# The second mixture's products move to GpSimd, two attention tiles at a time, and a repeated listing of the woven stages

## Chip, core and metric

One Trainium2 chip, one of its cores. The metric is the device time of one execution in microseconds (us); lower is better. The engines are TensorE (PE), VectorE (DVE), ScalarE (ACT), GpSimd (POOL) and SyncE (SP), which issues the DMAs here.

## The reference, cut to what matters

Four sequences (b = 0 to 3) of 1024 tokens of 128 numbers, in float32. Two layers:

```
xn = layernorm(x)
x  = x + attention0(xn) + mixture0(xn)            # 1 causal head; 16 experts of 64 + 1 shared, top 2
xn = layernorm(x)
x  = x + attention1(xn) + block1(xn)              # attention1: 16 heads of 8, not causal
# block1: res = xn + small causal attention (16 heads of 4) @ w_up
#         result = res + mixture1(rmsnorm(res))   # 8 experts of 256, top 2
mixture(t) = sum over experts of  route[t, e] * ((silu(t @ wg[e]) * (t @ wu[e])) @ wd[e])
attention0(t): softmax(t @ R @ t.T, causal) @ t
```

## The kernel before, in words

The tokens of a sequence are 8 tiles of 128 (T = 8) or two halves of 512 (HALF). For each sequence the program has two kinds of stages.

*The windows* (`Plan.windows`): eight groups of four heads, scores and exponentials and values. They are not touched by the change.

*The woven stages* (`Weave`, between two windows): here run together the tiles of the first attention and the first mixture of sequence b (`tiles`, `mixture` with which = 0), the closing of sequence b-1 (`closing`: output projections, residual, routing of the second mixture), the second mixture of sequence b-1 (`mixture` with which = 1), and the opening of the second layer of sequence b (`opening`: sums, norm, q, k, v, their bfloat16 parts written to DRAM, stacks read back, then the 32 "pieces" of the first head group with a row maximum each, the maxima split on GpSimd and placed by DMA, and then the first unit of the window). Stage 0 has no closing and no second mixture; the last stage has only a closing and a second mixture.

The program of each engine is written out at build time. `Weave` holds operations with an engine, an assumed duration and what they follow; `run` lists them: of those that can start within 0.1 us of the earliest, it takes the one with the longest tail of work behind it, and appends it to its engine's queue. A queue runs in that order; only semaphore waits hold an instruction.

*A step of a mixture* (18 for the first, 32 for the second): `gate` (PE, L1515; bank 0 or 3 in turn), its Tanh or Silu (ACT, L1284 or L1286) into `sg`, `up` (PE, L1525; one bank, U_BANK), the gated value `gu` (DVE, L1018 and L1024, or L1029 for the second mixture), the product `hid = gu * spread_w` with the route weights of one expert spread over the partitions (DVE, L1041), and `down` (PE, L1490), which adds into Y_BANK. `sg`, `gu` and `hid` have two buffers each; `spread_w` has four, filled by SP's DMAs (L777 for the second mixture) from `scratch_r`, where the routes were stored (L767). After each half `mixed` adds Y_BANK to x or writes `res` (L1054, L1056). The PE's `gate` of step 0 or 1 of a mixture waits in the kernel before for the gated value of the step in front of it:

```
                elif n >= 2:
                    pe.wait_ge(s["sg_ready"], k - 1)
                elif k:
                    pe.wait_ge(s["gu_ready"], k)
```

*A tile of the first attention* is a chain: scores (PE, L1435 and a mask, L1436), row maximum (DVE, L974), Exp with its sum (ACT, L1266), transposes (PE, L1441), their copy (ACT, L1272), values (PE, L1447), scaled add into x (DVE, L984). All of it passes through one PSUM tensor, FRONT_PS = ps[3], so the scores of tile t wait for L984 of tile t-1. The closing uses the PSUM tensor XA = ps[2], from its first transposes (L1648) over L1654, L1663, L1474, L1675 to the projection (L1680), which DVE adds to x (L1211), then the bias (L1214). The opening's split of q and k is L1070 (DVE) and L1293 (ACT).

## Time and profile before

| | us |
|---|---|
| runs | 2183.12, 2181.83, 2180.65 (median 2181.83) |
| the profiled execution | 2177.56, with a span of 2175.7 |
| PE busy | 2039.7 (94%) |
| DVE busy | 1549.5 (71%) |
| ACT busy | 1214.4 (56%) |
| GpSimd busy | 131.7 (6%) |
| stage 0 (span 0 to the first unit of a window) | 0 to 181.2 |
| woven stages 1, 2, 3 | 494.5 to 700.6, 1017.6 to 1223.4, 1540.5 to 1746.2 |
| last stage | 2058 to 2175.7 |

How to read it: busy time is the union of an engine's instructions; the span is from the first to the last instruction. An engine at 94% is near its end, but the share is a mean over stages, so each stage has to be looked at by itself.

### The profile page before, as it was taken

How to read it: one execution, taken by the hardware profiler on the slowest of the kernel's cores; microseconds unless marked ns; L12 is line 12 of the kernel's file. 1: busy time of each engine (PE TensorE's matmuls, PEld its weight loads, DVE VectorE, ACT ScalarE, POOL GpSimd, SP SyncE). 2: the span in 40 equal slices, each digit the busy share in tenths (PEclk: the TensorE clock that was granted, in tenths of full speed). 3: DMA queues.
4: the chain of work that ended last, by engine and by line, in shares of the span. 5: the costliest groups of instructions: out<-in, count | busy, mean ns of one | idle time of the engine just before them, and what ended most of it. 6: DMA issues, size and time to landing. Idle time of an engine off the chain costs nothing. (4 is left out here: it accounts for less than half of the span.)

```text
span 2175.7 us, 33722 instructions
## 1 busy us (share of the span) xinstructions
PE 2039.7 (94%) x11936; PEld 945.4 (43%) x11936; DVE 1549.5 (71%) x2807; ACT 1214.4 (56%) x2325; POOL 131.7 (6%) x251
## 2 busy tenths in 40 slices
PE   6869999989999999998989999999999999999889
PEld 4622333436665233344655423343565632334355
DVE  5678887746788887663779888774577988777155
ACT  2224777773532677776351467777444166777621
POOL 2000011100000000110000000110000000111000
PEclk9957999999999999999999999999999999999989
DMA  5160101002171100001145010010106301000011
GB/s 191 35 174 1 30 16 38 20 2 69 45 193 35 30 16 25 17 17 31 49 123 130 11 30 16 26 31 2 60 20 184 74 17 20 22 25 17 2 47 41
DMA packets 66632, 105.17 MB, mean 48 GB/s; under 512 B 11137, under 2 KB 20289, under 8 KB 66081
## 3 DMA queue, kind: packets, MB, share of 16 engines
q1 hardware_dynamic: 66464, 103.03, 17.6%
q8 instruction: 94, 1.54, 0.3%
q14 instruction: 74, 0.60, 0.1%
HBM read 79.26 MB, written 22.94 MB: 47 GB/s over the span
## 5 line engine op out<-in xcount | busy, mean ns | idle before, releaser
L1339 ACT ACTIVATE prob<-ps 128x512 f32<-128x512 f32 (+3 forms) x1792 | 867.4, 555 | 354.6 <-PE ps L1605 265.0
L1145 DVE TENSOR_REDUCE row_max<-ps 128x1 f32<-128x1024 f32 x512 | 606.6, 1219 | 106.3 <-PE ps L1574 105.6
L1605 PE MATMUL ps<-q_stack,k_stack 96*128 96x512 bf16 (+4 forms) x1792 | 553.0, 363 | 24.9 <-ACT prob L1339 17.0
L1574 PE MATMUL ps<-k_stack,q_stack 96*128 96x512 bf16 (+4 forms) x1792 | 534.9, 372 | 28.0 <-DMA q_stack<-scratch_q 15.6
L1142 DVE CUSTOM_DVE_ANT_0 tmp<-ps,const_b 128x128 f32<-128x128 f32 (+7 forms) x512 | 371.4, 756 | 131.3 <-PE ps L1574 118.1
L1630 PE MATMUL ps<-prob,v_ones 128*32 128x512 f32 (+3 forms) x3584 | 436.9, 559 | 2.5 <-ACT prob L1339 2.5
L1605 PEld LDWEIGHTS ps<-q_stack,k_stack 96*128 96x128 bf16 (+1 forms) x1792 | 172.5, 98 | 360.8 <-ACT prob L1339 231.8
L1574 PEld LDWEIGHTS ps<-k_stack,q_stack 96*128 96x128 bf16 (+1 forms) x1792 | 152.8, 99 | 376.3 <-DVE row_max L1142 94.9
L1490 PEld LDWEIGHTS ps<-wd,prob 128*128 128x128 f32 (+1 forms) x1600 | 207.1, 193 | 78.0 <-issue 66.3
L1286 ACT ACTIVATE prob<-ps 128x512 f32<-128x512 f32 x128 | 76.4, 597 | 288.5 <-PE ps L1515 287.9
L1490 PE MATMUL ps<-wd,prob 128*128 128x128 f32 (+1 forms) x1600 | 213.2, 278 | 3.3 <-DVE prob L1041 3.3
L1041 DVE TENSOR_TENSOR prob<-prob,spread_w 128x512 f32<-128x512 f32 x192 | 131.9, 688 | 52.2 <-PE ps L1490 50.5
L1515 PE MATMUL ps<-tT,wg 128*128 128x512 f32 x256 | 136.8, 617 | 14.1 <-DVE prob L1029 14.1
L1525 PE MATMUL ps<-tT,wu 128*128 128x512 f32 x256 | 134.6, 608 | 0.0
L1630 PEld LDWEIGHTS ps<-prob,v_ones 128*32 128x32 f32 x3584 | 70.6, 108 | 136.3 <-ACT prob L1339 75.9
L1029 DVE TENSOR_TENSOR prob<-prob,ps 128x512 f32<-128x512 f32 x128 | 87.4, 683 | 31.5 <-issue 12.6
L1607 PE MATMUL ps<-const_b 128*128 128x128 bf16 x512 | 103.5, 219 | 0.0
L1160 DVE RECIPROCAL rsum_g<-ps 128x16 f32<-128x16 f32 x64 | 16.5, 258 | 120.1 <-PE ps L1640 115.6
L1284 ACT ACTIVATE prob<-ps 128x512 f32<-128x512 f32 (+1 forms) x72 | 42.9, 596 | 82.5 <-PE ps L1515 81.7
L1515 PE MATMUL ps<-xT,wg 128*128 128x512 f32 x144 | 74.3, 598 | 0.3 <-DVE prob L1024 0.3
L1515 PEld LDWEIGHTS ps<-tT,wg 128*128 128x128 f32 x256 | 47.8, 194 | 56.9 <-issue 49.9
L853 POOL TENSOR_SCALAR m_rest<-row_max 128x32 f32<-128x32 f32 x32 | 9.3, 292 | 1041.9 <-DVE row_max L1145 849.8
(169 smaller groups left out, 1510.3 us busy)
## 6 DMA issues: line engine op xcount, KB each, us to landing
spread_w<-scratch_r SPq DMA_DIRECT2D x128, 128.0 KB, 2.9
spread_w<-scratch_r SPq DMA_DIRECT2D x64, 256.0 KB, 3.5
k_stack<-scratch_k SPq DMA_DIRECT2D x48, 256.0 KB, 6.8
q_stack<-scratch_q SPq DMA_DIRECT2D x48, 256.0 KB, 7.7
scratch_k<-tmp SPq DMA_DIRECT2D x36, 256.0 KB, 2.8
k_stack<-scratch_k SPq DMA_DIRECT2D x96, 64.0 KB, 2.2
q_stack<-scratch_q SPq DMA_DIRECT2D x96, 64.0 KB, 2.3
scratch_k<-tmp SPq DMA_DIRECT2D x36, 128.0 KB, 2.8
```

The lines of the kernel that those rows point to most:

```text
L1029: dve.tensor_tensor(gu[k % 2][0:m, :], sg[k % 2][0:m, :], bank(U_BANK)[0:m, :], ALU.mult).then_inc(s["gu_ready"], 1)
L1041: dve.tensor_tensor(hid[k % 2][:], gu[k % 2][:], spread_w[load % SPREADS][:], ALU.mult).then_inc(s["hid_ready"], 1)
L1142: dve.tensor_tensor_reduce(masked[r % 2][:, 0:keys], ring_pair(r)[:, 0:keys], mask_wide[:, S - keys:], 1.0, -3e38, ALU.add, ALU.max, nm[G ...
L1145: dve.tensor_reduce(nm[G % 2][:, t, j:j + 1], ring_pair(r)[:], AX_X, ALU.max).then_inc(s["ring_used"], 1)
L1339: act.activation(p_slot(v, j)[:, lo - at:hi - at], bank(UNIT_BANKS[u % 3])[:, 0:hi - lo], ACT.Exp, scale=SCALES[kind_of(G)]).then_inc(s["p ...
L1490: ins = pe.matmul(bank(Y_BANK)[:, t * D:(t + 1) * D], hid[k % 2][0:m, t * P:(t + 1) * P], wd[0:m, c * D:(c + 1) * D], start=(c, t) == (0, ...
L1515: pe.matmul(bank(G_BANKS[n % 2])[0:m, :], wg[:, c * P:c * P + m], xT[:, tok], start=True, stop=True).then_inc(s["gate_psum"], 1)
L1525: pe.matmul(bank(U_BANK)[0:m, :], wu[:, c * P:c * P + m], xT[:, tok], start=True, stop=True).then_inc(s["up_psum"], 1)
L1574: ins = pe.matmul(ring_pair(r)[:, lo:hi], queries(G, j)[:, t * P:(t + 1) * P], keys(G, j)[:, lo:hi], start=True, stop=True)
L1605: ins = pe.matmul(dst[:, 0:hi - lo], keys(G, j)[:, kc * P:(kc + 1) * P], queries(G, j)[:, lo:hi], start=True, stop=True)
L1607: ins = pe.matmul(dst[:, 0:P], mask_q, ident_b, start=False, stop=True, skip_group_check=True)
L1630: ins = pe.matmul(bank(V_BANK)[CW * j:CW * (j + 1), lo - at:hi - at], v_st[G % 2][:, kc, j, :], p_slot(v, j)[:, lo - at:hi - at], start=kc ...
```

## The change

1. The products of the second mixture (`spread` with which = 1) are issued by GpSimd, not by DVE. The first mixture's stay on DVE. They are in GpSimd's queue beside `maxima` and `stage_v`.
2. Tiles 0 to 3 of the first attention use the two halves of FRONT_PS in turn, tiles 4 and 6 all of FRONT_PS, tiles 5 and 7 all of XA. Tile t then waits for the tile that last had its space (`TILES_FREE`); tile 5 also for the closing of sequence b-1 to be done with XA (`po_used`, `rt_ready`). The transposed probabilities go back into the tile's own buffer `p0[t % 2]`.
3. `Weave.run` lists the operations up to 12 times, forwards and, from the ends so found, backwards, whose starts are the next turn's priorities; the best modelled end is kept. The plan is told of the engine and 1.1 us for the products, of shorter times for several PE operations, and of waits of the second mixture's first steps one by one (gate 0, gate 1, first product and first down each behind what they need of the first mixture, not all behind its last `mixed`).
4. In the program, `gate` of step 0 or 1 waits for the gated value of the step before the one in front of it, which frees its bank, its `sg` buffer being free then too.

The core of the diff (a few assumed times of `closing` and `opening`, and `heads`, are left out):

```diff
+    def listed(self, after, value):
+
+        waiting = [len(list_) for list_ in after]
+        follows = [[] for _ in self.ops]
+        for k, list_ in enumerate(after):
+            for d in list_:
+                follows[d].append(k)
+        at, free, out = [0.0] * len(self.ops), {}, []
+        can = [k for k, n in enumerate(waiting) if n == 0]
+        while can:
+            start = {k: max(at[k], free.get(self.ops[k][0], 0.0)) for k in can}
+            first = min(start.values())
+            k = max((k for k in can if start[k] <= first + 0.1), key=lambda k: (value[k], -k))
+            engine, _, took, _, lands = self.ops[k]
+            can.remove(k)
+            out.append((k, start[k]))
+            free[engine] = start[k] + took
+            for n in follows[k]:
+                at[n] = max(at[n], start[k] + took + max(lands, self.ops[n][4] if after is not self.after else 0.0) + (LAT if self.ops[n][0] != engine else 0.06))
+                waiting[n] -= 1
+                if not waiting[n]:
+                    can.append(n)
+        return out, max(start + self.ops[k][2] + self.ops[k][4] for k, start in out)
...
+    def run(self, plan, turns=12):
+
+
+        ops = self.ops
+        self.after = [sorted(set(op[3])) for op in ops]
+        follows = [[] for _ in ops]
+        for k, list_ in enumerate(self.after):
+            for d in list_:
+                follows[d].append(k)
+        value = [0.0] * len(ops)
         for k in reversed(range(len(ops))):
-            tail[k] += ops[k][2] + ops[k][4]
-            for d in ops[k][3]:
-                tail[d] = max(tail[d], tail[k] + LAT)
-        while len(self.end) < len(ops):
-            heads = [(max(at, self.free.get(ops[k][0], 0.0)), k) for at, k in self.heads()]
-            first = min(heads)[0]
-            _, k = max((tail[k], -k) for at, k in heads if at <= first + 0.1)
-            start = next(at for at, n in heads if n == -k)
-            self.free[ops[-k][0]] = self.place(plan, -k, start)
+            value[k] = ops[k][2] + ops[k][4] + max([LAT + value[n] for n in follows[k]], default=0.0)
+        best = None
+        for _ in range(turns):
+            out, end = self.listed(self.after, value)
+            if best is None or end < best[1]:
+                best = out, end
+            ends = [0.0] * len(ops)
+            for k, start in out:
+                ends[k] = start + ops[k][2] + ops[k][4]
+            back, _ = self.listed(follows, ends)
+            for k, start in back:
+                value[k] = start + ops[k][2]
+        for k, start in best[0]:
+            self.free[ops[k][0]] = self.place(plan, k, start)
...
+    def tiles(w, b, closed=None):
+
+        valued = []
         def do(engine, stage, took, *after):
             return w.op(engine, ("front", b, stage), took, *after)
-        used = do("ACT", "encode", 1.1, do("PE", "encode", 2.0))
-        out = []
+        coded = do("ACT", "encode", 1.1, do("PE", "encode", 1.73))
+        out, before = [], [None] * 7
         for t in range(T):
-            top = do("DVE", f"scores{t}", 0.15 + 0.13 * (t + 1), do("PE", f"scores{t}", 0.1 + 0.24 * (t + 1), used))
-            p = do("ACT", f"scores{t}", 0.45 + 0.115 * (t + 1), top)
-            turned = do("ACT", f"turn_p{t}", 0.18 + 0.115 * (t + 1), do("PE", f"turn_p{t}", 0.12 * (t + 1), p))
-            used = do("DVE", f"values{t}", 0.65, do("PE", f"values{t}", 0.25 * (t + 1), turned))
-            out.append(used)
+            freed = [out[t - 2]] if t >= 2 and t != 5 else []
+            if t == 4:
+                freed.append(out[3])
+            elif t == 5:
+                freed.append(closed)
+            at = [do("PE", f"scores{t}", 0.1 + 0.24 * (t + 1), coded, *freed, before[0])]
+            at.append(do("DVE", f"scores{t}", 0.15 + 0.13 * (t + 1), at[0], before[1]))
+            at.append(do("ACT", f"scores{t}", 0.45 + 0.115 * (t + 1), at[1], before[2], valued[t - 2] if t >= 2 else None))
+            at.append(do("PE", f"turn_p{t}", 0.12 * (t + 1), at[2], before[3]))
+            at.append(do("ACT", f"turn_p{t}", 0.18 + 0.115 * (t + 1), at[3], before[4]))
+            valued.append(do("PE", f"values{t}", 0.25 * (t + 1), at[4], before[5]))
+            out.append(do("DVE", f"values{t}", 0.65, valued[-1], before[6]))
+            before = at + [valued[-1], out[-1]]
         return out
...
-                at = do("PE", "gate", 0.88, last(taken, 2), last(taken) if n == 1 else None, last(scaled, 2), last(ups), xT if n == 0 else None, *(freed if n == 0 else ()))
+                at = do("PE", "gate", 0.865, last(taken, 2), last(scaled, 2), last(ups), xT if n == 0 else None, freed[n] if freed and n < 2 else None)
                 gates.append(do("ACT", "gate", 0.6, at, last(scaled, 2), last(gates)))
-                ups.append(do("PE", "up", 0.0 if which == 0 and n % C0 == C0 - 1 else 0.88, at, last(scaled), mixed if n == 0 else None))
+                ups.append(do("PE", "up", 0.0 if which == 0 and n % C0 == C0 - 1 else 0.865, at, last(scaled), freed[1] if freed and n == 0 else None))
...
-                hids.append(do("DVE", "spread", 0.7 if at else 0.05, scaled[-1], last(downs), last(hids), *at))
+                hids.append(do(("DVE", "POOL")[which], "spread", (0.7, 1.1)[which] if at else 0.05, scaled[-1], last(downs), last(hids), freed[2] if freed and n == 0 else None, *at))
...
-                downs.append(w.op("PE", ("down", b, which, n - 1), 1.05, hids[n - 1], last(out), last(downs)))
+                downs.append(w.op("PE", ("down", b, which, n - 1), 0.9, hids[n - 1], last(out), last(downs), freed[3] if freed and n == 1 else None))
...
-        return out, (taken[-1], scaled[-1], hids[-1], out[-1]), loads
+        return out, (scaled[-2], scaled[-1], downs[-1], out[-1]), loads
...
-        tiled = tiles(w, b)
+        tiled = tiles(w, b, project)
         mixed, freed, loads = mixture(w, b, 0, None, None if b else stored, (None, None), loads)
         if b:
-            mixture(w, b - 1, 1, xT, routed, (joined, joined), loads, freed, mixed[-1])
+            mixture(w, b - 1, 1, xT, routed, (joined, joined), loads, freed)
...
+        def tile_ps(t):
+
+            if t < T // 2:
+                return FRONT_PS[:, t % 2 * HALF:(t % 2 + 1) * HALF]
+            return (FRONT_PS, XA)[t % 2][:]
+
+        TILES_FREE = [0, 0, 1, 2, 4, 4, 5, 6]
...
+            def spread(b, which, n):
+                k, load = plan.step0[b, which] + n, plan.load_of(b, which, n)
+                if n == 0:
+                    pool.wait_ge(s["hid_ready"], k)
+                pool.wait_ge(s["gu_ready"], k + 1)
+                pool.wait_ge(spread_loaded[load % SPREADS], spread_count(load))
+                pool.wait_ge(s["down_done"], k - 1)
+                pool.tensor_tensor(hid[k % 2][:], gu[k % 2][:], spread_w[load % SPREADS][:], ALU.mult).then_inc(s["hid_ready"], 1)
+
             for what, *how in plan.of("POOL"):
-                if what == "maxima":
+                if what == "spread" and how[1] == 1:
+                    spread(*how)
...
-                    dve.tensor_reduce(nmax0[:, t:t + 1], FRONT_PS[:, 0:(t + 1) * P], AX_X, ALU.max, negate=True).then_inc(s["max0_ready"], 1)
+                    dve.tensor_reduce(nmax0[:, t:t + 1], tile_ps(t)[:, 0:(t + 1) * P], AX_X, ALU.max, negate=True).then_inc(s["max0_ready"], 1)
...
+                    if t >= 2:
+                        act.wait_ge(s["o0_psum"], b * T + t - 1)
+                    act.activation(p0[t % 2][:, 0:keys], tile_ps(t)[:, 0:keys], ACT.Exp, bias=nmax0[:, t:t + 1],
                                    accum_out=sum0[:, t:t + 1]).then_inc(s["p0_ready"], 1)
...
-                    act.activation(pT0[:, 0:keys], FRONT_PS[:, 0:keys], ACT.Copy).then_inc(s["pt_ready"], 1)
+                    act.activation(p0[t % 2][:, 0:keys], tile_ps(t)[:, 0:keys], ACT.Copy).then_inc(s["pt_ready"], 1)
...
-                    else:
-                        pe.wait_ge(s["o0_used"], b * T + t)
+                    if TILES_FREE[t]:
+                        pe.wait_ge(s["o0_used"], b * T + TILES_FREE[t])
+                    if b and t == T // 2 + 1:
+                        pe.wait_ge(s["po_used"], b)
+                        pe.wait_ge(s["rt_ready"], b)
...
-                elif k:
-                    pe.wait_ge(s["gu_ready"], k)
+                elif k >= 2:
+                    pe.wait_ge(s["gu_ready"], k - 1)
```

## Rows read from the trace of the kernel before

**Rows 1.** Windows by stage: length, engines busy (x instructions), granted clock, DMA share, GB/s.

```profile
0.00:181.20 181.20, 134.31 (x545) 70.21 (x546) 122.24 (x207) 42.67 (x65) 15.88 (x19) 0.80 0.41 120
494.50:700.60 206.10, 196.92 (x984) 127.48 (x983) 159.32 (x274) 70.38 (x107) 3.44 (x8) 0.98 0.33 89
1017.60:1223.40 205.80, 196.92 (x992) 127.41 (x991) 159.77 (x275) 70.38 (x107) 3.43 (x8) 0.98 0.34 89
...
2058.00:2175.70 117.70, 101.48 (x474) 66.28 (x472) 59.98 (x119) 27.85 (x43) 0.00 (x0) 0.92 0.15 41
```

**Rows 2.** Windows inside woven stage 1: tiles and first mixture, then opening, then pieces.

```profile
494.50:572.50 78.00, 76.69 (x424) 53.44 (x423) 55.15 (x122) 28.16 (x51) 0.00 (x0) 1.00 0.18 55
572.50:620.00 47.50, 39.93 (x185) 24.25 (x183) 33.95 (x68) 26.14 (x31) 1.33 (x1) 0.93 0.51 145
620.00:700.60 80.60, 80.29 (x377) 49.79 (x378) 70.23 (x85) 16.08 (x25) 2.11 (x7) 0.98 0.38 89
```

**Rows 3.** Waits of PE in woven stage 1: total us, times, longest.

```profile
PE ps L1515 <- DVE prob L1029: 4.4, 1, 4.4
PE ps L1574 <- DMA q_stack<-scratch_q: 3.0, 1, 3.0
PE ps L1424 <- DVE routeT L1007: 1.3, 1, 1.3
PE ps L1680 <- ACT tmp L1379: 0.3, 1, 0.3
```

**Rows 4.** Timeline of woven stage 1: start, length, engine, line, xcount, idle before.

```profile
539.80 1.56 PE L1435 MATMUL ps<-xT,tmp 128*128 128x512 f32 x4
...
573.62 2.05 PE L1680 MATMUL ps<-wo,tmp 128*128 128x128 f32 x16 [0.25 <-ACT tmp L1379]
...
575.51 1.02 PE L1525 MATMUL ps<-tT,wu 128*128 128x512 f32 x2
...
580.93 2.05 PE L1515 MATMUL ps<-tT,wg 128*128 128x512 f32 x2 [4.40 <-DVE prob L1029]
...
592.33 0.68 DVE L1041 TENSOR_TENSOR prob<-prob,spread_w 128x512 f32<-128x512 f32 x1
```

**Rows 5.** Windows behind PE's waits in stages 1 and 2 (columns as before).

```profile
580.93:587.42 6.49, 6.49 (x20) 3.39 (x21) 1.93 (x3) 3.22 (x5) 0.00 (x0) 0.54 0.04 5
1105.10:1111.50 6.40, 6.26 (x22) 3.17 (x23) 2.78 (x3) 4.08 (x6) 0.00 (x0) 0.73 0.04 5
...
620.10:624.00 3.90, 3.88 (x13) 2.45 (x14) 2.94 (x3) 0.60 (x1) 0.00 (x0) 0.62 1.05 196
```

**Rows 6.** Line of the row maxima in woven stage 1: durations in ns, first and last start.

```profile
L1145 DVE TENSOR_REDUCE row_max<-ps x33: 1212/1217/1225, 620.8 to 700.5; 128x1 f32<-128x1024 f32 x33
```

**Rows 7.** GpSimd's lines, ns minimum, median, maximum; one copy with DVE beside it.

```profile
L846 POOL COPY v_ones<-v_tok x16: 398/402/1330, 113.5 to 1852.2; 128x256 f32<-128x256 f32 x16
L857 POOL TENSOR_TENSOR m_rest<-m_rest,m_parts x32: 244/247/532, 174.0 to 2017.6; 128x32 f32<-128x32 f32 x32
...
595.76 2.55 DVE L1070 TENSOR_TENSOR tmp<-tmp 128x1024 f32<-128x1024 f32 x2
...
595.91 1.33 POOL L846 COPY v_ones<-v_tok 128x256 f32<-128x256 f32 x1 [145.42 <-DVE v_tok L1103]
```

**Rows 8.** Timeline of the last stage: closing, first product and down, one steady step.

```profile
2058.75 1.96 PE L1648 MATMUL ps<-const_f,v_tok 128*64 128x128 f32 x16 [0.61 <-DVE v_tok L1163]
...
2090.56 1.23 DVE L1214 TENSOR_TENSOR x<-x,bias_vo 128x1024 f32<-128x1024 f32 x1
...
2091.70 0.68 DVE L1041 TENSOR_TENSOR prob<-prob,spread_w 128x512 f32<-128x512 f32 x1
...
2092.53 2.05 PE L1490 MATMUL ps<-wd,prob 128*128 128x128 f32 x8 [3.33 <-DVE prob L1041]
...
2105.73 0.69 DVE L1041 TENSOR_TENSOR prob<-prob,spread_w 128x512 f32<-128x512 f32 x1 [1.11 <-PE ps L1490]
...
2109.76 1.05 PE L1490 MATMUL ps<-wd,prob 128*128 128x128 f32 x8
```

**Rows 9.** Window of the tiles and first mixture in stage 0 (same columns).

```profile
24.00:97.00 73.00, 69.25 (x360) 46.42 (x358) 48.30 (x93) 24.30 (x44) 0.34 (x1) 1.00 0.22 73
```

More of the change, by code:

```diff
@@ L297, in op @@
         return len(self.ops) - 1
-    def heads(self):
-        for k in [k for todo in self.todo.values() for k in todo]:
-            engine, item, took, after, lands = self.ops[k]
-            if all(d in self.end for d in after):
-                yield max([0.0] + [self.end[d] + self.ops[d][4] + (LAT if self.ops[d][0] != engine else 0.06) for d in after]), k
     def place(self, plan, k, at):
@@ L1226, in _ @@
                     up(*how)
-                elif what == "spread":
+                elif what == "spread" and how[1] == 0:
                     spread(*how)
```

29 lines of the change are left out of this document (13 added, 16 removed).

## Prediction

> **What bounds the kernel now.** I read the windows by stage first [rows 1], because the page's 94% for PE is a mean over stages. The change touches only the woven stages, stage 0 and the last stage. Woven stages 1 to 3 last about 206 us each, PE is busy in 196.9 us of that and its granted clock is 0.98; DVE is busy in 159.3 and ACT in 70.4. So PE sets the length of a woven stage, and what can be won is PE's idle time, 206.1 - 196.9 = 9.2 us a stage, and what its lower clock costs. Stage 0 has a lower mean clock and much more idle time, but most of that lies in its opening, a chain the change doesn't shorten.
>
> Inside stage 1 [rows 2] the first part, tiles and first mixture, keeps PE busy for 76.7 of 78.0 us at full clock. The last part, pieces and second mixture, keeps it busy for 80.3 of 80.6. All that is missing is in the middle: 39.9 of 47.5 us. PE's waits name it [rows 3]: 4.4 us in which a gate matmul (L1515) waits for the gated value L1029, and 3.0 us in which the first piece waits for its stack from DRAM; these two, with 1.3 and 0.3 and smaller ones, are the 9.2. Stages 2 and 3 show the same pattern. The timeline has the first place [rows 4]: the up matmul starts at 575.51 and lasts 1.02, then nothing until 580.93. The gate is step 1's and its wait (`gu_ready, k`) is for step 0's value, which DVE had behind the routing, the projection and the norm.
>
> A wait of PE costs more than itself. The gate that follows takes 2.05 us where the up before it took 1.02, and in the 6.49 us behind the wait the granted clock is 0.54 in stage 1, and 0.73 over 6.40 us in stage 2 [rows 5]: PE went from 2.4 to 1.2 GHz after it had idled and came back while it was kept busy. The loss is length times (1 - clock): 6.49 x 0.46 = 3.0 us and 6.40 x 0.27 = 1.7 us. Behind the wait for the stack it is 3.90 x 0.38 = 1.5 us.
>
> What is not the bound: the chain of the opening. The pieces start at 620.8 [rows 6]; 32 maxima of 1.217 us are 39 us, and some 10 us of splitting and placing follow, so the first unit could start near 670. It starts at 700.6, because PE does the second mixture in between. This chain has 30 us of room.
>
> **The change part by part.** *Products to GpSimd.* DVE loses 32 products of 0.69 us [rows 8], 22 us a stage. In the last part of the stage DVE is busy in 70.2 of 80.6 us, yet PE hardly waits there [rows 2], so this alone gives nothing there; in the middle part it takes a few products out of the queue in which L1029 stands. What one costs on GpSimd the trace doesn't show. From below: a copy of 256 columns takes 402 ns and a product of 32 columns 247 ns [rows 7], 0.69 ns a column, so 512 columns take 0.247 + 480 x 0.00069 = 0.58 us if a second input is free. From above: the copy's whole time, doubled for the columns and again for the second input, 1.61 us. I take 1.15, between the two. Is it hidden? In the steady step of the last stage a product starts at 2105.73, when the down two steps earlier has freed its buffer, and is used by the down at 2109.76 [rows 8]: ends of 2106.42 now and 2106.9 then are both early, with 2.9 us left; at 1.61 still 2.4. GpSimd needs 1.15 of each 2.61 us step. Behind the product in GpSimd's queue stand the six small instructions of `maxima`, for which the first unit waits; a product ahead of them costs at most 1.15 us once, in the chain with 30 us of room. SP's loads now wait for GpSimd's products instead of DVE's; four buffers and 2.61 us steps cover half a microsecond.
>
> The Trainium skill (GPSIMD Engine Reference, Elementwise — side-by-side cycle accounting) gives GpSimd about 2.6 cycles an element for a product of two inputs and 4497 ns for 2048 columns; the estimate for 512 columns is 1.1 us, and the sum would be the same by it.
>
> *Contention.* The copy of 402 ns took 1330 beside two L1070, DVE instructions that read two SBUF tensors; these took 2.55 us together instead of 2 x 1.216 [rows 7]; it happened in 4 of the 16 copies, once a stage. So a GpSimd instruction waited 0.93 us and DVE 0.1 to 0.2 us. The second mixture's products will meet DVE's two-input instructions of the opening (six L1070, six for the rotation, bias and join: 14). None of them is on PE's path as long as PE has other work, and the opening's chain has 30 us of room: I take 0. Uncovered, 14 delays of at most one product are 14 x 1.15 = 16 us a stage. The row maxima and L1029 read PSUM, and no copy beside them was longer than 404 ns.
>
> *Gates as banks need.* The gate of step 1 (0.86 us of PE time, a third of the 2.61 us step) no longer waits for L1029; of the 4.4 us it can fill 0.9. The next thing that is late is up 1, which still needs it, so the rest has to come from the order. From below this part is worth 0.9 us a stage, from above the wait and its low clock, 7.4 in stage 1.
>
> *Tiles.* Two at a time they no longer wait for each other. In stages 1 to 3 PE has no idle time there [rows 2], so nothing is won directly. But XA must be free before tile 5. Before, tile 5's scores began at 539.80, and the projection, which ends the closing, only at 573.62 [rows 4]. The closing alone takes from 2058.75 to 2090.56 [rows 8], 31.8 us, so it can be done by 494.5 + 31.8 = 526.3 if it is let go first; the new plan must put it ahead of tile 5. Then the second mixture's routes, whose first product was at 592.33 [rows 4], are known some 20 to 30 us earlier, and DVE's routing work no longer stands in front of L1029. That is what takes the 4.4 us away, together with a listing that sees PE's load (the backward pass counts it, the tail of the old one doesn't). In stage 0 [rows 9] PE idles 3.75 us in this part; I take 1.5 of it, bounds 0 and 3.75.
>
> *The wait for the stack* (3.0 us and 1.5 of low clock) is a DMA chain that the plan assumes too short; the edit doesn't aim at it. PE stalls only because the piece stands too early in its queue. I take a third: bounds 0 and 4.5.
>
> *The last stage.* The first product stood behind the bias add on DVE: it started at 2091.70, and PE waited 3.33 us for it [rows 8]. On GpSimd it starts when the spread weights are there, near 2089.7, and ends near 2090.9, 1.5 us earlier than 2092.4. The last product is 0.5 us later, and the down, the add and the store follow it. Net -1.0; the other 31 steps are PE's 2.61 us each and don't change.
>
> **The sum.** Wait: 3 x 4.4 = 13.2. Low clock behind it: 3.0 + 1.7 + 1.7 (stage 3 like 2) = 6.4. Stack: 3 x 1.5 = 4.5. Stage 0: 1.5. Last stage: 1.0. Together 26.6 us. The profiled execution took 2177.56 around its span of 2175.7 and would take 2151.0; it lies 4.3 below the median of the runs shown, 2181.83, which becomes 2155.2.
>
> **The rivals.**
> *More than that:* the new listing leaves PE no idle time. Then a stage gives all 9.2 and the clock (3.0 + 1.5 in stage 1, 1.7 + 1.5 in the others): 13.7 + 12.4 + 12.4 = 38.5, with 3.75 and 1.5: 44, so 2138. For it: all of PE's waits have other work that could fill them. Against it: first steps of the mixture still wait for routes, and DMA times stay off the plan.
> *Only the gate moves:* the order around the opening stays as it is, the wait shrinks by 0.9 and the clock falls as before. 3 x 0.9 + 1.0 = 3.7, so 2178, which counts as no change. For it: the chain of the opening is what a listing by tails puts first, and it is the same chain.
> *The shared reads:* DVE's opening is slowed by the products, and the wait for L1029 comes back in part. At 5 us a stage it takes 15 from 26.6: 2170. It would be slower than before only from 8.9 us a stage on. For it, the 1330 ns copies; against it, the 30 us of room.
> The Trainium skill (SBUF — State Buffer, Who interferes with whom) has this as a rule: a DVE instruction with two SBUF inputs and a GpSimd instruction that reads SBUF exclude each other, and the later one waits for the whole of the first. By that rule, the trace agrees, at 1.33 against 0.40 us.
> *Slower, tile 5 behind the closing:* if the closing isn't advanced, tile 5 starts when the projection has been added, the routes turned and copied, about 586 in place of 539.8. Tiles 5 to 7 took from 539.8 to 571, 31 us, so the opening would start at 617, 45 us late, of which 30 are room: 15 us a stage, 3 x 15 = 45 less the 1.0 and 1.5: 2224. It decides from a closing that ends later than about 570. Against it: the closing needs 32 us and has 75.
>
> **How the numbers follow.** Chances: forecast 0.48, more 0.18, only the gate 0.14, shared reads 0.10, tile 5 0.10. The range from 2130 to 2182 leaves out the slower case, the upper third of the gate case and a little below. This kernel's measurement tells about 0.2% (4.4 us) from no change. Faster by more than that (under 2177.5): 0.47 + 0.18 + 0.04 + 0.08 = 0.77. Within: 0.10. Slower: 0.13, tile 5 and some of the others.
>
> **What the profile after would show.** Woven stages near 198 us in place of 206, PE's wait for L1029 gone or under 1 us and no stretch near 0.54 behind it; the projection L1680 before the scores of tile 5, and the first product of the second mixture well before 97 us into the stage; 128 products on GpSimd at 0.6 to 1.6 us, longer beside L1070; the wait for the stack still there; windows of the same length; 2.61 us steps at the end. I am wrong if PE waits in the first part of a stage (for L1211 or L1376: tile 5), if a product takes more than 3 us, or if the listing puts queues in an order whose assumed times are off, so that many small PE waits take the place of one.

## The result, and the profile after

The changed kernel takes 2161.85 us (median of 4 runs, 2159.74 to 2163.9) against 2181.24 for the kernel before, timed beside it: a ratio of 0.9915, with a 95% interval of 0.99 to 0.9929, or 18.5 us less, between 15.5 and 21.8. I had forecast 2155.2, in a range of 2130 to 2182, by a gain of 26.6. The side is right, and the gain is 8 us short.

The profiled execution after took 2163.9 us with a span of 2162.0, the longest of its four, so the two spans differ by 13.7 us only. Here are its stages, as windows with the columns of [rows 1]: stage 0, woven stages 1, 2 and 3, the last stage.

```profile
0.00:182.90 182.90, 133.91 (x546) 70.03 (x547) 122.68 (x207) 42.85 (x65) 15.88 (x19) 0.80 0.41 119
494.80:695.20 200.40, 193.79 (x989) 125.23 (x988) 144.97 (x244) 70.26 (x107) 44.13 (x40) 1.00 0.33 92
1011.80:1215.70 203.90, 198.37 (x989) 127.81 (x987) 145.23 (x244) 70.15 (x107) 44.03 (x40) 0.97 0.33 90
1531.40:1731.80 200.40, 193.80 (x990) 125.27 (x989) 145.05 (x244) 70.27 (x107) 44.13 (x40) 1.00 0.34 92
2042.40:2162.00 119.60, 104.61 (x475) 68.28 (x473) 39.40 (x87) 27.84 (x43) 41.53 (x32) 0.90 0.13 40
```

Cut at the same instructions in both traces (the table below says which; [rows 1] is cut up to 0.8 us off them), the woven stages are 6.5, 1.7 and 5.5 us shorter (13.7 in all), stage 0 is 1.2 longer, the last stage 1.8 longer, and the four windows are 0.1, 0.7, 1.2 and 1.0 shorter. Stage 0, the last stage and the windows cancel each other, so the span too is 13.7 shorter. In stage 1 PE is busy 3.1 us less than before, in stage 3 it is 2.6, and in both its clock is 1.00 in place of 0.98. DVE is busy 14.4 us less in stage 1 and GpSimd 40.7 us more. In stage 2 PE's busy time rose by 1.5 us and its clock is 0.97.

Inside stage 1 the three parts of [rows 2] show which one changed (same columns):

```profile
494.80:576.50 81.70, 80.35 (x456) 56.65 (x455) 60.42 (x136) 31.36 (x54) 0.00 (x0) 1.00 0.21 66
576.50:621.00 44.50, 40.42 (x192) 25.10 (x191) 31.20 (x51) 25.07 (x31) 14.50 (x11) 1.00 0.47 136
621.00:695.20 74.20, 73.02 (x344) 43.47 (x342) 53.35 (x58) 13.82 (x22) 29.63 (x30) 1.00 0.38 93
```

The middle part had 7.6 us of idle PE before and has 4.1 now, at a clock of 1.00 instead of 0.93. PE's waits in this stage (total us, times, longest):

```profile
PE ps L1587 <- DVE prob L1086: 2.4, 2, 1.7
PE ps L1577 <- issue: 1.4, 1, 1.4
PE ps L1636 <- DMA q_stack<-scratch_q: 0.8, 1, 0.8
PE ps L1623 <- DVE tmp L1186: 0.8, 1, 0.8
PE ps L1552 <- POOL prob L918: 0.6, 1, 0.6
```

The 4.4 us in which a gate waited for the gated value [rows 3] are gone, and the stack's 3.0 are 0.8. What is new is that `up` (L1587) waits, twice, together 2.4 us: 0.72 us in step 1, which the timeline shows, and 1.73 in a later step, at 607.2.

```profile
576.07 1.12 PE L1577 MATMUL ps<-tT,wg 128*128 128x512 f32 x2
577.03 1.02 PE L1587 MATMUL ps<-tT,wu 128*128 128x512 f32 x2
577.89 1.02 PE L1577 MATMUL ps<-tT,wg 128*128 128x512 f32 x2
578.88 0.69 DVE L1086 TENSOR_TENSOR prob<-prob,ps 128x512 f32<-128x512 f32 x1
579.63 1.13 PE L1587 MATMUL ps<-tT,wu 128*128 128x512 f32 x2 [0.72 <-DVE prob L1086]
```

Gate 0, up 0, gate 1 follow each other, and up 1 waits 0.72 us for what took 4.40 before [rows 4]. The order of the closing has changed as forecast too: the projection (L1742) now runs at 532.2, and the scores of tile 5 come behind it. GpSimd's first product of the stage starts at 579.7, not at 592.33 [rows 4]. The timeline's row of tile 5, then the rows by line (ns minimum, median, maximum; first and last start):

```profile
543.52 1.45 PE L1497 MATMUL ps<-xT,tmp 128*128 128x512 f32 x4
```

```profile
L1742 PE MATMUL ps<-wo,tmp x16: 273/275/275, 532.2 to 533.8; 128*128 128x128 f32 x16
...
L918 POOL TENSOR_TENSOR prob<-prob,spread_w x128: 1261/1266/2246, 579.7 to 2156.0; 128x512 f32<-128x512 f32 x128
```

All of this looks like the prediction's reason come true: DVE starts the first gated value (L1086) 0.8 us after the first `up` has ended, where it took 3.6 us in the kernel before. The experiments show that the gain doesn't need it: with the closing as late as before, the time is as good or better.

### The profile page after: what moved, and what is told of

It is laid out like the page before. It is cut to its first block, busy times and chain, and to the rows that moved or that the text cites. A ratio compares the mean times of both kernels' runs of the same rounds, so it can differ in the third digit from the quotient of the medians.

```text
span 2162.0 us, 33753 instructions
## 1 busy us (share of the span) xinstructions
PE 2038.4 (94%) x11936; PEld 944.3 (44%) x11936; DVE 1485.4 (69%) x2679; ACT 1215.9 (56%) x2325; POOL 294.9 (14%) x379
## 4 chain that ended last, share of the span: by engine, by line
PE 83%; DVE 5%; ACT 3%; DMA 2%; issue 2%; POOL 1%; SPq 1%; POOLq 0%; DVEq 0%; ACTq 0%
PE ps L1692 19%; PE ps L1667 17%; PE ps L1636 16%; PE ps L1552 7%; PE ps L1587 6%; PE ps L1577 6%; DVE row_max L1202 3%; PE ps L1702 2%; ACT prob L1398 1%; DMA q_stack<-scratch_q 1%; PE ps L1509 1%; PE ps L1497 1%; PE ps L1669 1%; PE ps L1475 1%; PE ps L1503 1%
## 5 line engine op out<-in xcount | busy, mean ns | idle before, releaser
L918 POOL TENSOR_TENSOR prob<-prob,spread_w 128x512 f32<-128x512 f32 x128 | 164.5, 1286 | 689.8 <-DVE prob L1086 511.7
L1086 DVE TENSOR_TENSOR prob<-prob,ps 128x512 f32<-128x512 f32 x128 | 87.3, 682 | 95.3 <-PE ps L1587 74.5
L1587 PE MATMUL ps<-tT,wu 128*128 128x512 f32 x256 | 135.7, 612 | 5.6 <-DVE prob L1086 5.6
L880 POOL MEMSET q_stack<- 128x4096 bf16 x16 | 56.2, 3512 | 223.7 <-PE ps L1667 149.0
```

The costliest lines, as they stand in the source:

```text
L918: pool.tensor_tensor(hid[k % 2][:], gu[k % 2][:], spread_w[load % SPREADS][:], ALU.mult).then_inc(s["hid_ready"], 1)
L1086: dve.tensor_tensor(gu[k % 2][0:m, :], sg[k % 2][0:m, :], bank(U_BANK)[0:m, :], ALU.mult).then_inc(s["gu_ready"], 1)
L1587: pe.matmul(bank(U_BANK)[0:m, :], wu[:, c * P:c * P + m], xT[:, tok], start=True, stop=True).then_inc(s["up_psum"], 1)
```

## The experiments

Every ratio is against the kernel before, timed beside it, with a 95% interval. The table has the stages of each profiled execution in us, each from the start of the last matmul of one window to the first unit of the next; these are single executions, and those of one kernel differ by 3 to 17 us, so only differences that repeat over stages or pairs are read.

| kernel | ratio | stage 0 | woven 1, 2, 3 | last |
|---|---|---|---|---|
| before | 1 | 181.7 | 206.9, 205.6, 205.9 | 117.8 |
| after | 0.9915 | 182.9 | 200.4, 203.9, 200.4 | 119.6 |
| e1 | 0.9943 | | | |
| e2 | 0.9897 | 184.2 | 197.9, 198.3, 197.9 | 120.5 |
| e3 | 0.9976 | 186.1 | 203.9, 205.1, 203.0 | 116.3 |
| e4 | 1.0013 | 182.9 | 209.7, 210.7, 206.2 | 120.8 |
| e5 | 0.9924 | 184.8 | 199.2, 198.8, 198.4 | 113.4 |
| e6 | 0.9967 | 180.3 | 202.3, 204.3, 201.4 | 118.0 |
| e7 | 1.0027 | 181.0 | 205.1, 205.5, 205.3 | 123.5 |
| e8 | 0.9888 | 186.2 | 197.9, 198.2, 197.9 | 114.9 |
| e9 | 0.9919 | 182.5 | 200.6, 204.8, 200.5 | 114.8 |
| e10 | 1.002 | 187.0 | 206.6, 207.9, 204.7 | 119.0 |
| e11 | 0.986 | 182.8 | 199.4, 198.0, 198.2 | 114.8 |
| e12 | 0.9897 | 182.5 | 200.9, 201.3, 199.0 | 113.4 |

### e1: the change with its products on DVE

```diff
-                hids.append(do(("DVE", "POOL")[which], "spread", (0.7, 1.1)[which] if at else 0.05, scaled[-1], last(downs), last(hids), freed[2] if freed and n == 0 else None, *at))
+                hids.append(do("DVE", "spread", 0.7 if at else 0.05, scaled[-1], last(downs), last(hids), freed[2] if freed and n == 0 else None, *at))
...
-                if what == "spread" and how[1] == 1:
-                    spread(*how)
-                elif what == "maxima":
+                if what == "maxima":
...
-                elif what == "spread" and how[1] == 0:
+                elif what == "spread":
```

> The changed kernel with the second mixture's products back on DVE, in the plan (0.7 us) and in the program; all else as changed. If the gain comes from the order (closing ahead of tile 5, listing backwards), the woven stages keep 3 to 6 us each of theirs and the last stage loses its collisions with the adds: about 2160, level with the changed kernel. If it comes from DVE's relief, L1029's wait comes back and the time goes to 2175 to 2181.

Measured: 0.9943 (0.9925 to 0.9962). Its profiled execution took 6180.75 us, where the three others took 2163.71 to 2169.9. In it the score matmuls of the windows (L1665) took 921 ns in the median, where they took 379 in the kernel before, with a granted clock of 1.00 on record; what it was I don't know, and no stage is read from it. Two thirds of the gain stay without GpSimd.

### e2: tiles one at a time, XA not needed

```diff
-            if t < T // 2:
-                return FRONT_PS[:, t % 2 * HALF:(t % 2 + 1) * HALF]
-            return (FRONT_PS, XA)[t % 2][:]
+            return FRONT_PS[:]
-        TILES_FREE = [0, 0, 1, 2, 4, 4, 5, 6]
+        TILES_FREE = list(range(T))
...
-                    if b and t == T // 2 + 1:
-                        pe.wait_ge(s["po_used"], b)
-                        pe.wait_ge(s["rt_ready"], b)
```

and `tiles` of the plan as before, with `encode` at 1.73.

> The changed kernel with one tile at a time through FRONT_PS as before, so that nothing forces the closing ahead of tile 5; listing, GpSimd's products and gates as changed. If the constraint of XA brings the closing forward, the time goes back to 2172 to 2180 and the projection comes after tile 5's scores again. If the backward listing does it, 2158 to 2165 and the projection stays early.

Measured: 0.9897 (0.9877 to 0.9917), 2156.83 us, no worse than the whole change. This is the experiment that shows that my reason isn't needed for the gain. Its stage 1 as a window, and then the line of the projection:

```profile
495.90:693.80 197.90, 193.05 (x989) 125.00 (x987) 143.89 (x244) 69.92 (x107) 44.93 (x40) 1.00 0.34 93
```

```profile
L1728 PE MATMUL ps<-wo,tmp x16: 273/275/275, 576.3 to 577.9; 128*128 128x128 f32 x16
```

The projection is as late as in the kernel before (576.3, with 573.62 in [rows 4]), 44 us later than in the changed kernel, and yet the stage is 2.5 us shorter. The time is that of the expectation's second case (a little better) and the late projection that of its first, so neither case holds whole. The gated value comes late here too: DVE starts it 5.9 us after the first `up` has ended. But PE doesn't wait for it, since the projection, gate 1, the routing's matmul and the norm's (L1457) stand in its queue between the two `up`s. PE's waits are small ones; the largest two are for the router's tensors:

```profile
PE ps L1457 <- ACT routeT L1424: 1.3, 1, 1.3
PE ps L1472 <- DVE routeT L1053: 1.3, 1, 1.3
```

### e3: the change with one listing

```diff
-    def run(self, plan, turns=12):
+    def run(self, plan, turns=1):
```

> The changed kernel with a single forward listing by tails (turns = 1), all else as changed. If the backward listing counts, woven stages of 203 to 206 us and 2172 to 2180; if the tiles' constraint or GpSimd do it alone, no more than 3 us above 2162.

Measured: 0.9976 (0.9963 to 0.9988). Without the repeats 0.6% of the 0.85% is gone. PE's waits in its stage 1:

```profile
PE ps L1587 <- DVE prob L1086: 3.9, 2, 3.2
PE ps L1636 <- DMA q_stack<-scratch_q: 2.8, 1, 2.8
```

The hole at gate 1 stays closed without the repeats: `up` 1 waits 0.71 us, as in the change. The 3.2 is in front of a later `up`, at 611.59, where the change has 1.73, and the stack's wait is back. These two are what the repeats shortened.

### e4: the kernel before with the repeated listing alone

`listed` and the new `run` of the change, whose core is:

```diff
+        for _ in range(turns):
+            out, end = self.listed(self.after, value)
...
+            back, _ = self.listed(follows, ends)
+            for k, start in back:
+                value[k] = start + ops[k][2]
...
-            _, k = max((tail[k], -k) for at, k in heads if at <= first + 0.1)
```

> The kernel before with nothing but the repeated listing. If the listing alone is worth most of the change, 2163 to 2170. If it needs the tiles' two places or GpSimd's products, 2176 to 2182.

Measured: 1.0013 (0.9998 to 1.0028). The same listing shows no gain where the plan and the gate's wait are the old ones; the wait of stage 1 is 4.9 us, not 4.4:

```profile
PE ps L1544 <- DVE prob L1058: 4.9, 1, 4.9
PE ps L1603 <- DMA q_stack<-scratch_q: 3.4, 1, 3.4
```

### e5: one tile at a time and products on DVE (the edits of e1 and e2 together)

> One tile at a time and the products on DVE: the repeated listing and the gates (in plan and program) are all that is left of the change. If these two carry the gain and GpSimd adds only what it did with two tiles (about 6 us), 2161 to 2164. If GpSimd carries most of it, 2172 or more and a wait for L1029's counterpart in the woven stages.

Measured: 0.9924 (0.9907 to 0.994). Only the listing, the plan's new times and the gates are left of the change, and they give nearly as much as all of it.

### e6: the kernel before with the gate's wait alone

```diff
-                elif k:
-                    pe.wait_ge(s["gu_ready"], k)
+                elif k >= 2:
+                    pe.wait_ge(s["gu_ready"], k - 1)
```

> The kernel before with nothing but the gate's wait in the program (for the gated value one step earlier); the order of every queue as before. If the gate can only fill 0.9 us of the hole and the clock falls all the same, woven stages 0.5 to 1.5 us shorter, 2177 to 2179. If that gate is enough to keep the clock up, 2.5 us shorter, 2172 to 2175.

Measured: 0.9967 (0.9954 to 0.998), 7.2 us; the order of every queue is that of the kernel before. Its woven stages are 4.6, 1.3 and 4.5 us shorter. The timeline around the place of [rows 4]:

```profile
574.62 1.02 PE L1525 MATMUL ps<-tT,wu 128*128 128x512 f32 x2
575.48 1.02 PE L1515 MATMUL ps<-tT,wg 128*128 128x512 f32 x2
578.35 1.04 PE L1474 MATMUL ps<-const_f,routes 128*8 128x128 f32 x8 [1.84 <-DVE routes L942]
579.23 0.69 DVE L1029 TENSOR_TENSOR prob<-prob,ps 128x512 f32<-128x512 f32 x1
579.97 1.13 PE L1525 MATMUL ps<-tT,wu 128*128 128x512 f32 x2 [0.59 <-DVE prob L1029]
```

One gate matmul now stands in the hole, and the routing's L1474, which had queued behind the gate, has come forward with it. What is left is 1.84 and 0.59 us. As windows, the hole and what is behind it:

```profile
576.50:580.00 3.50, 1.07 (x10) 0.64 (x9) 3.40 (x15) 3.46 (x5) 0.00 (x0) 1.00 0.00 0
580.00:587.00 7.00, 7.00 (x23) 3.53 (x24) 4.43 (x5) 3.41 (x5) 0.00 (x0) 1.00 0.36 119
```

1.00 behind the hole, where [rows 5] had 0.54. The clock stayed at 2.4 GHz over a stretch in which PE was busy for 1.07 of 3.50 us. Stage 3 has the same waits and no fall behind them either. Stage 2 has them too (1.87 and 0.58), with the same matmuls between, and there the clock fell all the same:

```profile
1096.00:1099.70 3.70, 1.59 (x10) 0.93 (x11) 3.67 (x13) 3.57 (x5) 0.00 (x0) 1.00 0.00 0
1099.70:1103.10 3.40, 3.40 (x12) 2.26 (x11) 2.35 (x3) 1.26 (x3) 0.00 (x0) 0.50 0.17 45
```

It fell a second time at 1116.8, after 6.8 us in which PE had not been idle at all. So the gate makes the hole smaller in every stage, by 2.0 us (0.9 for itself, the rest for the L1474 that it had held up), and what the clock gives back differs: PE is busy 2.7 and 1.4 us less in stages 1 and 3, and 1.6 more in stage 2, which is why that stage is only 1.3 us shorter.

### e7: the kernel before with GpSimd's products alone

```diff
-                hids.append(do("DVE", "spread", 0.7 if at else 0.05, scaled[-1], last(downs), last(hids), *at))
+                hids.append(do(("DVE", "POOL")[which], "spread", (0.7, 1.1)[which] if at else 0.05, scaled[-1], last(downs), last(hids), *at))
```

and the `spread` of the change in GpSimd's program.

> The kernel before with nothing but the second mixture's products on GpSimd (plan 1.1 us, and program). If DVE's relief works by itself, 2168 to 2175; if the hole at the gate stays because the plan holds the second mixture behind the first, 2177 to 2184, with 1.27 us a product and the last stage some 2 us longer.

Measured: 1.0027 (1.0013 to 1.0042): alone, the move that gives the change its name makes the kernel slower. PE's waits, the first of its stage 1, the second of its last stage:

```profile
PE ps L1526 <- DVE prob L1040: 4.4, 1, 4.4
...
PE ps L1501 <- POOL prob L872: 4.1, 3, 1.9
```

DVE with 22 us less of products answers no sooner, because what stands in front of the gated value isn't products. In this profile the woven stages are 0.1 to 1.8 us shorter; it is the last stage that is longer, 123.5 us with 117.8, at a clock of 0.89 with 0.92.

### e8, e9: the last stage's products on DVE, in e2 and in the change

```diff
-                hids.append(do(("DVE", "POOL")[which], "spread", (0.7, 1.1)[which] if at else 0.05, scaled[-1], last(downs), last(hids), freed[2] if freed and n == 0 else None, *at))
+                hids.append(do("POOL" if which and b < B - 1 else "DVE", "spread", (1.1 if which and b < B - 1 else 0.7) if at else 0.05, scaled[-1], last(downs), last(hids), freed[2] if freed and n == 0 else None, *at))
...
-                if what == "spread" and how[1] == 1:
+                if what == "spread" and how[1] == 1 and how[0] < B - 1:
...
-                elif what == "spread" and how[1] == 0:
+                elif what == "spread" and (how[1] == 0 or how[0] == B - 1):
```

> One tile at a time, and of the second mixture's products those of the last stage (sequence 3) on DVE, the others on GpSimd. If the products and the bias and residual adds hold each other up in the last stage, it shortens from 120.5 to 117 or 118 us and the time to about 2154, the best so far. If not, the last stage stays at 120.

> The changed kernel, two tiles at a time, with the last stage's products on DVE. If GpSimd's products cost the last stage 3 to 5 us, 2156 to 2159 on the scale where before is 2180, ratio 0.989 to 0.990. If the last stage's length is only where the clock falls, no difference from the changed kernel (0.9915).

Measured: e8 0.9888 (0.9871 to 0.9904) beside e2's 0.9897; e9 0.9919 (0.9899 to 0.994) beside the change's 0.9915. In the profile the last stage is 5.6 and 4.8 us shorter, of which 1.4 and 1.0 are idle time of PE and the rest is busy time at another clock (0.92 with 0.88 and 0.90); in the times nothing is certain. e8 beside e9 is the tiles question again, with the same answer as e2 beside the change.

### e10: e8 with the old wait of the gate

The edit of e6 reversed; the plan and every order are those of e8.

> e8 (one tile, repeated listing, new plan, last products on DVE) with the old wait of gate 1 in the program. If the wait is what held PE, the hole before the gate comes back with the clock at half behind it, woven stages 2 to 5 us longer, ratio 0.991 to 0.996 (e8: 0.9888). If the new order has already put the value ahead of the gate, no difference.

Measured: 1.002 (1.0012 to 1.0029), more than the 0.991 to 0.996 expected. One wait takes the whole gain away, 0.0132 or 29 us. In stage 1 the timeline has the place, and then the window behind it:

```profile
587.64 2.04 PE L1563 MATMUL ps<-tT,wg 128*128 128x512 f32 x2 [4.96 <-DVE prob L1075]
```

```profile
587.60:595.00 7.40, 6.21 (x19) 3.65 (x20) 2.26 (x2) 4.07 (x6) 0.00 (x0) 0.50 0.04 7
```

5.0 us of waiting and 7.40 x 0.50 = 3.7 us of clock are 8.7 us; the stage is 206.6 - 197.9 = 8.7 us longer. That the two agree to the tenth is chance, since the fall lasts until 595.8, past the window, and e8 has two small waits in this place. Over the whole stage PE is idle 5.3 us longer than in e8 and busy 3.4 us longer. Over the three stages that is 16.6 and 8.6 us: two thirds of what the wait costs is waiting, and one third is PE's work taking longer at the lower clock.

### e11, e12: the order of stage 0, and all products on DVE in it

In the change's stage 0 the DVE line that forms q and k from their sums, `qk_c` (L1173), stands ahead of the third split of q and k (L1127), the reverse of the order before. The timeline of after:

```profile
117.79 1.23 DVE L1173 TENSOR_TENSOR tmp<-ps,rstd_c 128x1024 f32<-128x1024 f32 x1 [1.42 <-PE ps L1617]
118.93 2.35 DVE L1127 TENSOR_TENSOR tmp<-tmp 128x1024 f32<-128x1024 f32 x2
```

The same place in the kernel before:

```profile
117.79 2.35 DVE L1070 TENSOR_TENSOR tmp<-tmp 128x1024 f32<-128x1024 f32 x2
```

The split starts 1.1 us later; the parts, their store and the stacks follow it, and PE's wait for the first stack in stage 0 is 8.4 us, where it was 7.0. e11 is e8 with the old order there; e12 is e11 with all products on DVE.

```diff
-        three = do("ACT", "third_parts", 2.0, do("DVE", "third_parts", 2.4, two))
+        third = do("DVE", "third_parts", 2.4, two)
+        three = do("ACT", "third_parts", 2.0, third)
...
-        qk = do("DVE", "qk_c", 1.3, do("PE", "qk_c", 1.8, c, v), vc)
+        qk = do("DVE", "qk_c", 1.3, do("PE", "qk_c", 1.8, c, v), vc, third if b == 0 else None)
```

> e8 with one more line in the plan: in stage 0 the addition of qk_c on DVE follows the third parts, as in the kernel before. If the new listing's stage 0 is longer because DVE waits for PE's slow matmuls with the third parts behind, stage 0 shortens from 184 to 186 us to 182 to 184 and the ratio goes to 0.988. If stage 0 varies by itself, nothing.

> e11 with all products of the second mixture on DVE, so that it differs from e11 only in the woven stages. By the profiles (198.8 against 198.0 us a stage) GpSimd is worth about 3 us: ratio 0.0015 above e11's. By the timed ratios (two tiles 0.9943 against 0.9915, one tile 0.9924 against 0.9897) it is worth 6 us or more: 0.003 to 0.004 above.

Measured: e11 0.986 (0.9842 to 0.9878), 2147.97 us, the fastest of all; its stage 0 is 182.8 us with 186.2 in e8, but 1.5 of these 3.4 us are there before the place of the swap (DVE forms v at 112.69 and at 114.24). e12 0.9897 (0.9884 to 0.9911), so GpSimd's products in the woven stages are worth 0.0037 or 8 us here, together with the order that the listing finds for them, since the plan's engine changes with the program's. The second woven stage of e11 and that of e12 as windows, and PE's wait there in e12, which e11 has not:

```profile
1009.10:1207.10 198.00, 193.12 (x989) 125.02 (x988) 143.87 (x244) 69.97 (x107) 44.99 (x40) 1.00 0.34 93
```

```profile
1011.20:1212.50 201.30, 195.01 (x992) 126.62 (x991) 160.11 (x276) 70.04 (x107) 3.52 (x8) 0.99 0.33 91
```

```profile
PE ps L1621 <- DMA q_stack<-scratch_q: 2.8, 1, 2.8
```

With 16 us less on DVE the opening's chain reaches DRAM earlier, and the first piece finds its stack. The three stages of e12 wait 2.5, 2.8 and 2.2 us for it.

## Why the prediction was right and wrong

**The place was right.** The idle time of the middle part set what could be won. The three terms of the woven stages, 13.2 + 6.4 + 4.5 = 24.1 us, are what e2 has in its profile: 9.0 + 7.3 + 8.0 = 24.3. The changed kernel got 13.7 of them.

**Part of the nearness is luck.** In the profile the terms came out at 13.7 for 24.1 (woven stages), -1.2 for 1.5 (stage 0) and -1.8 for 1.0 (last stage), and 3.0 us came from the windows, where I had nothing: 13.7 for 26.6. The times have 18.5, partly because the profiled execution before (2177.56) was faster than the median of its kernel and the one after the slowest of its four. The range of 52 us would have held a much smaller gain as well.

**The step that was wrong in its weight: "That is what takes the 4.4 us away".** I gave the wait's end to the closing, which XA's new use forces ahead of tile 5, and to the listing; the gate's own new wait I put between "0.9 a stage" and 7.4 and counted at nothing of its own. The projection did move by 41 us. The routes' loads start 25 us earlier (L823 at 563.1, L777 at 587.9 before), as forecast, and the first product 13, since it then waits for the gated value. But e2 keeps the projection late and is as fast or faster, so the closing is one way to lose the wait and not the only one, nor the better. Without it the gate's wait decides: alone, in the old order, its release gives 7.2 us (e6), and taking it back in e8's order costs 29 (e10). I counted the 0.86 us of one matmul that fills the hole, and missed two things. The routing's matmul stood behind the gate in PE's queue and came forward with it, so the hole shrank by 2.0 us a stage and not by 0.9. And in stages 1 and 3 of e6 the clock no longer fell behind it. The rival "only the gate moves" had the same faults and gave 3 x 0.9 = 2.7 for the gate, for what measured 7.2.

What the gate's release is worth inside the changed kernel itself, where the closing is early, no run shows. By the rows of its stage 1 the old wait would have held gate 1 until the gated value was done at 579.57, some 1.6 us in place of the 0.72 in front of `up` 1: about 0.9 us a stage, an estimate, if the clock stays up. Nor was the plan's part (the shorter times, and the first steps' waits one by one) ever tried without the rest.

As for the clock, a wait of 4.4 to 5.0 us in front of a gate had a fall behind it in each stage of before, e4, e7 and e10, though not one of fixed size: [rows 5] has 0.54 over 6.49 us in stage 1 and 0.73 over 6.40 in stage 2. The Trainium skill (TensorE: Matmul & The Clock Gate, Why this matters for your kernels) has this as advice, to leave no long idle gap between bursts of matmuls, because the engine falls to its lower clock behind it. By that rule, the trace agrees, at 0.54 behind 4.40 us. The shorter gaps went both ways: those of 1.8 and 0.6 us in e6 were followed by 1.00 in stages 1 and 3 and by 0.50 in stage 2, and in e11 the same two waits of 0.65 and 1.34 us by 0.51 over 3.5 us in stage 1 and by 1.00 in stage 2. The stretch of 3.7 us with them has PE busy for 1.74 us in the first case and 1.71 in the second. So releasing the gate made the fall rarer, and didn't rule it out; what decides between the two is open.

**The tiles.** "Nothing is won directly" holds, but I expected an indirect gain and there is a loss. Three pairs differ by the tiles alone: 0.9915 and 0.9897 (after, e2), 0.9943 and 0.9924 (e1, e5), 0.9919 and 0.9888 (e9, e8): each time two at a time is 0.2 to 0.3% slower. No single pair's intervals are apart, all three have the same sign. In the profiles it is 2.5, 5.6 and 2.5 us in the woven stages of after, and 2.7, 6.6 and 2.6 of e9; the 2.4 us in front of two `up`s and 1.4 of issue in after's stage 1 are not in e2's. Stage 2 loses more because of the clock, which is 1.00 over all of e2's. It fell twice in after's: behind the stack's wait (PE's wait of stage 2, then the window behind it), and before that at 1117.0, behind a stretch in which PE was busy throughout (the last two windows):

```profile
PE ps L1636 <- DMA q_stack<-scratch_q: 2.1, 1, 2.1
```

```profile
1140.00:1146.00 6.00, 6.00 (x21) 3.13 (x19) 4.50 (x5) 0.60 (x1) 1.26 (x1) 0.72 1.06 206
...
1110.00:1117.00 7.00, 7.00 (x37) 4.25 (x37) 5.15 (x6) 5.07 (x6) 1.32 (x1) 1.00 0.47 181
1117.00:1123.80 6.80, 6.80 (x21) 4.51 (x21) 5.43 (x5) 0.01 (x1) 1.37 (x1) 0.50 0.32 123
```

The falls cost 6.00 x 0.28 = 1.7 and 6.80 x 0.50 = 3.4 us, together 5.1 of the 5.6. Against stage 1 of the same kernel, which has no fall, PE idles 1.1 us less in stage 2, and the stage is 3.5 us longer. e9 has both falls in the same places. What brought the one at 1117.0 is open, and so is whether it belongs to two tiles: e6, with one tile, has such a one. Which wait or order of two tiles costs the 2.5 us of stages 1 and 3 was only read in the profiles, not tried. The rival "tile 5 behind the closing" did not happen: the closing was advanced, as its condition asks.

**The listing.** I named it half a sentence, as a helper. It is worth 0.6% inside the change (e3) and nothing clear of noise alone (e4). e4 lacks the new plan as well as the gate's release; that the release is needed is shown by e10, where listing and plan are the new ones and the gain is gone: while gate 1 waits for gated value 0, PE's queue stops there whatever stands behind it.

**The stack.** "I take a third", 1.5 a stage. In stages 1 and 3 of after 2.2 us of wait and 1.5 of clock went, so about 3.7 of 4.5; in stage 2 little. e3, e5 and e12 show what it takes: with one listing, or with the products back on DVE, the wait is 2.1 to 2.8.

**GpSimd.** The product takes 1.266 us (1.15 taken, bounds 0.58 and 1.61): my value was 0.12 low, and no wait hangs on the 0.12. The lower bound's price of 0.69 ns a column was drawn from a copy and a product, which don't share a fixed part; two copies of the same trace (292 ns for 128 columns, 402 for 256) have 0.86. "This alone gives nothing there" is confirmed by e7's stage 1, with its wait still 4.4. Its value comes in the new order: 0.3 to 0.4% (e1 and after, e5 and e2, e12 and e11).

**Contention, taken as 0.** This was too low in the last stage. I forecast it 1.0 us shorter, and the profile shows it 1.8 longer, though the first product does start 2.5 us earlier in the stage. The timeline there, and then PE's wait for the products:

```profile
2073.29 1.28 DVE L1268 SCALAR_TENSOR_TENSOR x<-ps,scale,x 128x1024 f32<-128x1024 f32 x1 [4.49 <-PE ps L1742]
2073.64 3.47 POOL L918 TENSOR_TENSOR prob<-prob,spread_w 128x512 f32<-128x512 f32 x2 [70.48 <-DMA spread_w<-scratch_r]
2074.60 1.39 DVE L1271 TENSOR_TENSOR x<-x,bias_vo 128x1024 f32<-128x1024 f32 x1
2075.06 1.13 PE L1552 MATMUL ps<-wd,prob 128*128 128x128 f32 x8 [1.81 <-POOL prob L918]
2076.03 2.17 DVE L1274 TENSOR_TENSOR x<-x,res 128x1024 f32<-128x1024 f32 x1
2077.17 2.08 PE L1552 MATMUL ps<-wd,prob 128*128 128x128 f32 x8 [0.98 <-POOL prob L918]
```

```profile
PE ps L1552 <- POOL prob L918: 4.1, 3, 1.8
```

Two products took 3.47 us instead of 2.53, and the second of two adds 2.17, where the bias add took 1.23 before [rows 8]. PE waited 4.1 us for products in three places, where it had waited 3.33 in one. Here the closing's DVE work is next to PE's path; in the woven stages it isn't. The collisions are there too: DVE's busy time in stage 1 fell by 14.4 us where 22 us of products had left it, and the six splits (L1127) took 1654 ns in the median and 2291 at most, where they had taken 1216. No wait of PE there is traced to it. The size in the last stage is open: in the profiles its products on DVE save 5 us, in the times (e8 beside e2, e9 beside after) the ratio is 0.0009 lower and 0.0004 higher. The last stage varies from 113.4 to 123.5 us between kernels, its clock between 0.88 and 0.94, and the clock alone could make up the 1.8: length times (1 - clock) is 12.0 us in after's last stage and 9.3 before.

The Trainium skill (SBUF — State Buffer, Who interferes with whom) says that a DVE instruction with two SBUF inputs and a GpSimd read exclude each other for a whole instruction. By that rule, these rows agree: 0.94 us lost in the two products, as much again in the add (2.17 us, where the same add had taken 1.22 before).

**Stage 0.** I forecast 1.5 us less from PE's idle time among the tiles, and it is 1.2 longer. I never asked what a new listing does to an order that was good: it swapped two DVE instructions in the chain to the stacks. e11's one dependence brings 0.9888 to 0.986, timed apart from each other; the intervals overlap, so the gain is likely and not certain. In the profiles about 1.9 of the 3.4 us of stage 0 lie behind the swap.

**The windows** were to stay as long as they were; they are 3.0 us shorter in sum in this profile. Over all kernels they vary by 1 to 4 us each with no edit to them, so I ascribe this to nothing.

## What to carry to other kernels

Price a stall of TensorE with the clock behind it, and a wait's release with all that stands behind it in the queue: letting a matmul of under 1 us go where the engine would idle for 4 to 5 was worth 3.5 us a stage in the old order (e6) and 8.4 in the new (e10 beside e8), as means of three stages. The clock's part is no fixed price: the wait of 4.4 us cost 3.0 us of it in one stage and 1.7 in the next [rows 5], and the two short waits of e6 cost 1.7 us in one stage and nothing in the two others. Before a new order is tried, release the waits in the program that are stricter than the buffers need; with the one in place the better order gave nothing (e10), and each of the two was worth a multiple with the other. A trace in which the forecast step comes true doesn't show that the gain needs it; here it took a run without the step (e2). Moving work off an engine that isn't the bound made the kernel slower alone and faster together with an order that used it, so such a part is judged inside the change and not by itself, and a new listing has to be read in every stage, those that it was not made for too.

## What the runs showed of the hardware

The granted clock stayed at 1.00 in e6 over a stretch of 3.50 us with 1.07 us of TensorE work and behind it, and fell to half (0.50 over 7.40 us in e10) around an idle time of 4.96. Behind 3.70 us with 1.59 of work, in e6's stage 2, it was 0.50 over 3.40 us. It was 0.72 over 6.00 us in after's stage 2, behind 6 us in which PE was busy for 3.94, and 0.50 over 6.80 us behind 7.00 in which it was busy throughout. A GpSimd product of two 128x512 float32 tensors in SBUF takes 1.266 us, 1.261 at least; a VectorE one 0.69. A product of 32 columns takes 0.247 us [rows 7] and one of 512 takes 1.266, so 2.1 ns a column with two inputs, about two and a half times the 0.86 of the copies.
